# A softmax bound from one column sum per half of the heads, and products with V kept in stock, in an attention and feed-forward kernel on eight cores

## The chip, the cores and the metric

The kernel runs on all eight cores of one Trainium2 chip (two dies of four cores). Each core runs the same program on its own data and none waits for another. The metric is the device time of the slowest core in microseconds (us). Of an execution with a profile, the span is the time from the first to the last instruction on the slowest core; the execution's own time is a little longer.

## What is computed

```python
def attn(x, Wc_down, Wq_up, Wkv_up, Wc_proj):      # 16 heads of 64, one shared K and V
    B, T = (4, 2048)                               # overwritten below: x is (2, 8192, 1024)
    Bsz, Tlen, C = x.shape
    latent = x @ Wc_down                           # 1024 -> 512
    q = (latent @ Wq_up).reshape(Bsz, Tlen, 16, 64)
    kv = latent @ Wkv_up
    k, v = (kv[..., :64], kv[..., 64:])
    att = jnp.einsum('bthd,bsd->bhts', q, k) / 8
    att = jnp.where(causal, att, -jnp.inf)
    att = jax.nn.softmax(att, axis=-1)
    y = jnp.einsum('bhts,bsd->bthd', att, v).reshape(Bsz, Tlen, C)
    return y @ Wc_proj

def ffn(x, w_gate, w_up, w_down):                  # int32 weights times 1/127, hidden 3072
    h = silu(x @ wg.T) * (x @ wu.T)
    return h @ wd.T

xn = layernorm(x)
out = x + attn(xn) * silu(ffn(xn))
```

## The kernel before

**Shares.** Cores 0 to 3 take the first batch row and cores 4 to 7 the second. A core normalizes all 8192 rows of its batch row in 64 tiles of 128 rows (L409, L413), turns them (L241 into `xnT`), and makes keys `kT` and values `vaug` from them in 16 groups of 512. Of each group it owns 128 queries, one **slot**; it computes attention for its 16 slots and the feed-forward part for the same 2048 rows, in four blocks of 512.

**Attention by units.** A slot has four head groups (`hg`) of four heads, and each runs over the keys so far in **units** of 256 keys: `full` ones, then two diagonal ones, `dA` and `dB`, which are multiplied by a mask. There are 1088 units. One unit is (1) scores, four matmuls into two PSUM banks, contraction over 64 rows, where the two halves of the array's rows work side by side (`ps<-qT,kT`, L940; all matmuls are recorded at the helper's line, L230); (2) one exponential on ScalarE, 128x1024, to a slot of the ring `p_sb` (six slots) or, for `dB`, `p_dg` (two slots) (L957); (3) for the diagonal ones the mask, on VectorE or GpSimd (L965); (4) the product with V, eight matmuls of 65 columns (`ps<-vaug,p_sb`, L990), all summed in bank 6. After the last unit of a head group VectorE divides (L1008, L1010), and the next head group's first product waits for that.

**The bound.** The exponential takes a bias per query and half of the heads, `nbias`, instead of a maximum found from the scores: minus a bound that comes from |q| and the greatest |k|. Per slot (`gen_q`) GpSimd squares the queries (L561); four matmuls of 512 columns with a matrix of ones in one half of its rows (`halves_sb`) sum them over partitions, one for each half of the heads and each partition half; VectorE takes the greatest of each (L570), then the greater of two (L582), and then does seven small operations (L583 to L592).

**Order of the work.** All orders are fixed when the program is built. A planner steps through the program in TensorE's order and keeps an estimated time for each engine. At each step it looks at what could come next: scores of two units, or three when a third pair of banks (4 and 5) is lent (`nbuf == 3`), which is done only when no other work is near; the product with V of the oldest unit; the generators in `work` (queries, keys and values, projections); and `lazy`, the feed-forward part. The first of them that is ready by the estimates is taken, in this order. LayerNorm and the ends of the feed-forward part run in the background, on the other engines. Banks 4, 5 and 7 serve all that is not attention (`take`, `give`). When all scores are out (`nu == NU`) the feed-forward part uses longer forms (`gen_down_alone`). Feed-forward weights come over rings: `wgu_sb` (three slots) and `wdr` (eleven).

## Time and profile before

| | us |
|---|---|
| median of 3 runs | 1488.38 (1488.12 to 1488.52) |
| execution with the profile | 1486.96 |
| its span, slowest core (0) | 1485.4; the other cores 1476.2 to 1483.6 |
| TensorE busy with matmuls | 1366.6 (92% of the span) |
| ScalarE busy | 1198.4 (81%) |
| VectorE busy | 690.0 (46%) |
| GpSimd busy | 198.6 (13%) |

Busy times of the engines overlap. A busy TensorE is not one at its peak, since the ends of matmuls are modelled and include what they wait for inside the pipeline. A row of the timeline merges equal instructions that follow each other; the time from its start to the start of the next row of the same engine says more than its length. Where a row names what ended an idle time, that is inferred from semaphores. Some matmul records are missing (of 144 in a row, 141 may stand).

### The profile page before, as it was taken

What the parts mean: (1) busy time and instruction counts of PE and PEld (TensorE: products, weight loads), DVE (VectorE), ACT (ScalarE), POOL (GpSimd) and SP (SyncE); (2) the same over time, 40 slices, a digit from 0 to 9 for tenths busy, and PEclk for the clock granted to TensorE, in tenths of its full rate; (3) what the DMA queues carried; (4) which work ended last, traced back from release to release, by engine and by line L of the source; (5) the groups of instructions that cost most, each with busy time, mean ns of one, the idle gap of its engine ahead of it and who ended that gap; (6) DMA issues with size and microseconds to landing.
All of it is one profiled execution on the core that took longest, in us unless ns stands there. A gap on an engine that the chain in (4) does not pass through costs nothing.

```text
span 1485.4 us, 44737 instructions; the slowest of 8 cores (1476.2 to 1485.4 us)
## 1 busy us (share of the span) xinstructions
PE 1366.6 (92%) x17929; PEld 799.7 (54%) x18064; DVE 690.0 (46%) x1321; ACT 1198.4 (81%) x1254; POOL 198.6 (13%) x352
## 2 busy tenths in 40 slices
PE   2689998899999899999998999999999899999998
PEld 2555555555555556555555555555555555555553
DVE  3678765677574535535334134333332323333325
ACT  3576676777879797997987997998999799998971
POOL 3322122222212212001001012000000112000000
PEclk9899999999999999999999999999999999999999
DMA  9825555476848463421221332421223043212113
GB/s 235 149 86 134 138 111 152 126 184 141 212 124 243 106 198 95 129 73 68 91 79 38 108 104 91 128 73 44 73 73 119 23 140 122 72 64 82 58 45 106
DMA packets 64762, 164.68 MB, mean 111 GB/s; under 512 B 7728, under 2 KB 15152, under 8 KB 64560
## 3 DMA queue, kind: packets, MB, share of 16 engines
q1 hardware_dynamic: 52272, 131.26, 27.3%
q0 software_dynamic: 12288, 30.54, 11.2%
q8 instruction: 149, 2.44, 0.7%
q14 instruction: 53, 0.43, 0.1%
HBM read 151.42 MB, written 33.55 MB: 125 GB/s over the span
## 4 chain that ended last, share of the span: by engine, by line
PE 74%; ACT 8%; issue 7%; DVE 5%; DMA 4%; POOL 1%; DVEq 0%; ACTq 0%; SPq 0%; POOLq 0%
PE ps L230 73%; ACT p_sb L957 6%; DMA h_sb<-wkv 2%; PE ps L241 2%; DVE bnd L570 1%; ACT p_dg L957 1%; POOL p_dg L965 1%; DMA wgub<-wgu_sb 1%; DMA xt<-xb 1%; DVE g_sb L708 1%; DMA wdr<-wd 1%; DVE xnT L473 0%; DVE xn L413 0%; ACT xnT L470 0%; ACT xn L409 0%
## 5 line engine op out<-in xcount | busy, mean ns | idle before, releaser
L957 ACT ACTIVATE p_sb<-ps,nbias 128x1024 bf16<-128x1024 f32 x1024 | 1064.0, 1124 | 150.3 <-PE ps L230 149.7
L230 PEld LDWEIGHTS ps<-vaug,p_sb 128*128 128x128 bf16 x8192 | 310.1, 97 | 190.9 <-issue 154.5
L230 PE MATMUL ps<-vaug,p_sb 128*128 128x65 bf16 x8192 | 386.7, 194 | 24.6 <-DVE p_sb L965 10.1
L230 PE MATMUL ps<-own_f,wgu_sb 128*128 128x512 bf16 x1536 | 393.3, 380 | 7.2 <-DVE g_sb L708 2.1
L230 PE MATMUL ps<-qT,kT 64*128 64x256 bf16 (+1 forms) x4352 | 331.5, 270 | 15.1 <-DVE xnT L473 4.1
L230 PEld LDWEIGHTS ps<-qT,kT 64*128 64x128 bf16 x4352 | 165.0, 94 | 218.7 <-issue 197.5
L230 PE MATMUL ps<-wdr,h_sb 128*128 128x512 bf16 x696 | 182.8, 380 | 5.6 <-DMA wdr<-wd 0.4
L230 PEld LDWEIGHTS ps<-own_f,wgu_sb 128*128 128x128 bf16 x1536 | 126.2, 97 | 109.5 <-issue 11.8
L708 DVE COPY g_sb<-ps 128x512 f32<-128x512 f32 x96 | 66.2, 690 | 190.7 <-PE ps L230 190.1
L710 ACT ACTIVATE t_sb<-g_sb 128x512 f32<-128x512 f32 x96 | 60.8, 634 | 55.3 <-DVE g_sb L708 51.3
L230 PEld LDWEIGHTS ps<-wdr,h_sb 128*128 128x128 bf16 x768 | 62.5, 98 | 50.5 <-issue 4.1
L723 DVE TENSOR_TENSOR h_sb<-g_sb,ps 128x512 bf16<-128x512 f32 x96 | 66.0, 688 | 49.0 <-PE ps L230 45.5
L720 DVE SCALAR_TENSOR_TENSOR g_sb<-t_sb,g_sb 128x512 f32<-128x512 f32 x96 | 66.3, 690 | 46.1 <-ACT t_sb L710 46.1
L965 DVE TENSOR_TENSOR p_sb<-p_sb,mask_sb 128x512 bf16<-128x512 bf16 x63 | 28.8, 456 | 119.5 <-ACT p_sb L957 119.5
L561 POOL TENSOR_TENSOR sq_sb<-qT 128x1024 bf16<-128x1024 bf16 x16 | 31.3, 1956 | 264.5 <-DVE qT L554 143.9
L241 PE MATMUL ps<-ident_sb,xn 128*128 128x128 bf16 x512 | 39.6, 227 | 25.8 <-ACT xn L409 16.4
L230 PE MATMUL ps<-wproj_sb,yT 128*128 128x512 bf16 x235 | 60.8, 379 | 1.1
L768 DVE COPY acc_sb<-ps 128x512 f32<-128x512 f32 x28 | 19.3, 690 | 88.3 <-PE ps L230 88.3
L873 POOL TENSOR_TENSOR acc_sb<-acc_sb,xo_t 128x512 f32<-128x512 f32 x24 | 30.3, 1261 | 177.9 <-DVE acc_sb L870 171.1
L965 POOL TENSOR_TENSOR p_dg<-p_dg,mask_sb 128x512 bf16<-128x512 bf16 x11 | 15.0, 1365 | 283.9 <-ACT p_dg L957 283.9
L241 PEld LDWEIGHTS ps<-ident_sb,xn 128*128 128x128 bf16 x512 | 32.1, 102 | 28.8 <-issue 27.5
L381 DVE BATCH_NORM_STATS2 st<-xt 128x6 f32<-128x512 f32 x57 | 38.9, 683 | 16.8 <-DMA xt<-xb 16.8
(100 smaller groups left out, 996.2 us busy)
## 6 DMA issues: line engine op xcount, KB each, us to landing
wgu_sb<-wgub SPq DMA_DIRECT2D x72, 512.0 KB, 3.4
xt<-xb SPq DMA_DIRECT2D x57, 512.0 KB, 6.0
wdr<-wdb SPq DMA_DIRECT2D x72, 256.0 KB, 3.7
wgu_sb<-wgu POOLq DMA_DIRECT2D x24, 512.0 KB, 7.7
wgub<-wgu_sb SPq DMA_DIRECT2D x24, 512.0 KB, 7.0
out<-acc_sb POOLq DMA_DIRECT2D x28, 256.0 KB, 3.5
wdr<-wd POOLq DMA_DIRECT2D x24, 256.0 KB, 8.4
wdb<-wdr SPq DMA_DIRECT2D x24, 256.0 KB, 8.1
```

What stands on the lines that cost most here:

```text
L230: return p.op("tensor", lambda e: e.matmul(out, lhsT, rhs, start=start, stop=stop, skip_group_check=shared), waits, "pe" if tok else None, ...
L241: return p.op("tensor", lambda e: e.transpose(out, in_, ident_sb[:, :]), waits, "pe" if tok else None, 56.0)
L381: V(600, lambda e, xs=xs, s6=s6: e.bn_stats(s6[:, 0:6], xs[:, 0:512]), [x_tok[j], nrm_tok.get(j - 8)])
L561: sq = P(2200, lambda en: en.tensor_tensor(sq_sb[:, :], qf, qf, ALU.mult), [qe, sq_free[0]])
L708: gc = V(690, lambda e, gv=gv, bg=bg: e.tensor_copy(gv, bank(bg)), [mm, g_free[gr]])
L710: th = A(480, lambda e, gv=gv: e.activation(t_sb[:, :], gv, AF.Tanh, scale=SIG / 2.0), [gc, t_free[0]])
L720: h1 = V(690, lambda e, gv=gv: e.scalar_tensor_tensor(gv, t_sb[:, :], 1.0, gv, ALU.add, ALU.mult), [th])
L723: h2 = V(690, lambda e, gv=gv, bu=bu, m=m: e.tensor_tensor(h_sb[:, m, :], gv, bank(bu), ALU.mult), [h1, mm] + h_free)
L768: accd[tt] = V(690, lambda e, av=av, bd=bd: e.tensor_copy(av, bank(bd)), [mm, acc_free[tt]])
L873: o = (V if over else P)(690 if over else 1200, lambda en: en.tensor_tensor(av, av, res, ALU.add), [u2, t_res])
L957: ex = A(cost, lambda en, dst=dst, src=src, bias=bias: en.activation(dst, src, AF.Exp, bias=bias, scale=0.125), [mm, p_prior(u)[1], bias_t ...
L965: ex = (V if on_v else P)(430 if on_v else 1150, lambda en, mk=mk: en.tensor_tensor(mk, mk, mask_sb[:, :].rearrange("p (a n) -> p a n", n= ...
```

## The change

The changed kernel does five things.

1. **One sum per half of the heads.** The matrix of ones is read shifted by 64 columns (`halves_sb[:, 64:192]`), so that one matmul of 512 columns gives the sum over the lower rows in one half of the output partitions and over the upper rows in the other. Two matmuls and two VectorE maxima per slot are left of four and four. The maxima are written in bfloat16 (`bndb`), and a matmul of two columns with an identity turned by 64 (`ident_sb[:, 64:192]`) exchanges the halves; VectorE then takes the greater of the two, reading PSUM. A factor 1.01 covers the rounding.
2. **Products with V in stock.** The product of the oldest unit is offered first only when five or more (`KEEP`) could run in a row, or the last unit of a head group is within reach. Otherwise it is offered after all other work and the feed-forward part.
3. **Single units.** Scores of one unit alone may be taken when the feed-forward part is done, or when (with two pairs of banks) the scores still to come, at 985 ns each, make more than the TensorE work that is left, with a margin of 40 us.
4. **Rings.** `p_sb` has seven slots instead of six, `wdr` ten instead of eleven.
5. The identity that is loaded is 64 columns wider.

```diff
-DR = 11
-PR = 6
+DR = 10
+PR = 7
+PE_WORK = 1195e3
+SPARE = 40e3
+KEEP = 5
...
             for half in range(2):
-                for o in range(2):
-                    yield lambda: max(ready(sq, t_hv), bank_t())
-                    b, fr = take()
-                    mm = MM(bank(b), halves_sb[:, o * 128:(o + 1) * 128],
-                            sq_sb[:, half * 512:(half + 1) * 512], True, True,
-                            [sq, t_hv] + fr, tok=True)
-                    red = V(690, lambda en, b=b, half=half, o=o: en.reduce_max(
-                        bnd[:, par, half * 2 + o:half * 2 + o + 1], bank(b), axis=AX.X),
-                        [mm, bnd_free[par]])
-                    give(b, [red])
+                yield lambda: max(ready(sq, t_hv), bank_t())
+                b, fr = take()
+                mm = MM(bank(b), halves_sb[:, 64:192], sq_sb[:, half * 512:(half + 1) * 512], True, True,
+                        [sq, t_hv] + fr, tok=True)
+                red = V(690, lambda en, b=b, half=half: en.reduce_max(
+                    bndb[:, par, half:half + 1], bank(b), axis=AX.X), [mm, bnd_free[par]])
+                give(b, [red])
             sq_free[0] = mm
-            yield lambda: ready(kmx_tok.get(e))
+
+            yield lambda: max(ready(red, kmx_tok.get(e)), bank_t())
+            b, fr = take()
+            turned = MM(bank(b)[:, 0:2], ident_sb[:, 64:192], bndb[:, par, :], True, True, [red, t_id] + fr, tok=True)
...
-            a = V(265, lambda en: en.tensor_tensor(pr, q2[:, :, 0], q2[:, :, 1], ALU.max), [red])
+            a = V(265, lambda en, b=b: en.tensor_tensor(pr, bank(b)[:, 0:2], bndb[:, par, :], ALU.max), [turned])
+            give(b, [a])
...
+            single = lazy.done or nbuf == 2 and (NU - nu) * 985.0 + SPARE > PE_WORK - p.pe_work + (NU - nu) * 100.0
...
-                    if n >= 2 and tn > t0:
+                    if n >= (1 if single else 2) and tn > t0:
...
-                if n >= 2 or n and (nu + n == NU or units[nu + n][0] > units[nu][0]):
+                if n >= 2 or n and (single or nu + n == NU or units[nu + n][0] > units[nu][0]):
                     offer(at, ("s", n))
-            if na < nu:
+
+            kept_av = 0
+            while na + kept_av < nu and av_t(na + kept_av) <= t0 and not units[na + kept_av][5]:
+                kept_av += 1
+            if na < nu and (kept_av >= KEEP or units[min(na + kept_av, NU - 1)][5]):
                 offer(av_t(na), ("v", na))
             for w in work:
                 offer(w.at(), ("w", w))
             if not lazy.done:
                 offer(lazy.at(), ("w", lazy))
+            if na < nu:
+                offer(av_t(na), ("v", na))
```

In the two built programs TensorE has 534 runs of score matmuls before (512 of two units, 21 of three, one of one) and 566 in the changed kernel (482, 20 and 64). When the product of a unit stands in TensorE's order, two or three younger units have been scored for 919 of the 1088 units before; in the changed kernel five or more for 588, and fewer than two for 40 (before: 144). Halfway through TensorE's work, counted by matmul columns (scores by half, since two run side by side), 528 units are scored before and 492 in the changed kernel; of the 2304 matmuls of the feed-forward part 920 are done before and 1016 in the changed kernel.

**First place: a diagonal pair in the middle of the program (about 722 us in the profile), on TensorE.** `ps<-qT,kT` are scores (a row of 128x128 is the `dB` unit), `ps<-vaug,p_sb` and `ps<-vaug,p_dg` products with V, `own_f,wgu_sb` and `wdr,h_sb` the two parts of the feed-forward part. Before:

```order
L230 MATMUL ps<-qT,kT 128x256 x8
L230 MATMUL ps<-vaug,p_sb 128x65 x16
L230 MATMUL ps<-own_f,wgu_sb 128x512 x8
L230 MATMUL ps<-qT,kT 128x128 x4
L230 MATMUL ps<-qT,kT 128x256 x4
L230 MATMUL ps<-vaug,p_sb 128x65 x16
L230 MATMUL ps<-qT,kT 128x256 x8
L230 MATMUL ps<-vaug,p_dg 128x65 x8
L230 MATMUL ps<-own_f,wgu_sb 128x512 x6
```

The same `dB` unit in the changed kernel:

```order
L237 MATMUL ps<-qT,kT 128x256 x4
L237 MATMUL ps<-qT,kT 128x128 x4
L237 MATMUL ps<-vaug,p_sb 128x65 x8
L237 MATMUL ps<-wdr,h_sb 128x512 x2
L237 MATMUL ps<-vaug,p_sb 128x65 x8
L237 MATMUL ps<-wdr,h_sb 128x512 x4
L237 MATMUL ps<-qT,kT 128x256 x8
L237 MATMUL ps<-vaug,p_sb 128x65 x40
L237 MATMUL ps<-qT,kT 128x256 x8
L237 MATMUL ps<-vaug,p_dg 128x65 x8
```

Before, the products of two units (16 matmuls) and one run of scores lie between the scores of the `dB` unit and its product; in the changed kernel the products of seven units, six matmuls of 512 columns and two runs of scores.

**Second place: the bound of the last slot (about 1169 us), on TensorE.** `sq_sb,halves_sb` are the sums, `bndb,ident_sb` the exchange. Before:

```order
L230 MATMUL ps<-vaug,p_sb 128x65 x16
L230 MATMUL ps<-sq_sb,halves_sb 128x512 x3
L230 MATMUL ps<-vaug,p_sb 128x65 x16
L230 MATMUL ps<-qT,kT 128x256 x12
L230 MATMUL ps<-sq_sb,halves_sb 128x512
L230 MATMUL ps<-vaug,p_sb 128x65 x8
L230 MATMUL ps<-wdr,h_sb 128x512 x4
```

In the changed kernel:

```order
L237 MATMUL ps<-sq_sb,halves_sb 128x512 x2
L237 MATMUL ps<-qT,kT 128x256 x4
L237 MATMUL ps<-vaug,p_sb 128x65 x8
L237 MATMUL ps<-own_f,wgu_sb 128x512 x2
L237 MATMUL ps<-qT,kT 128x256 x4
L237 MATMUL ps<-vaug,p_sb 128x65 x8
L237 MATMUL ps<-bndb,ident_sb 128x2
L237 MATMUL ps<-own_f,wgu_sb 128x512 x2
L237 MATMUL ps<-qT,kT 128x256 x4
```

The row of three units (x12), which needs banks 4 and 5, stood between the sums and is gone from here; single units stand around the sums, and the exchange comes two units after them.

**Third place: the end of the program, on TensorE.** `wproj_sb,yT` is the projection of the last slot. Before:

```order
L230 MATMUL ps<-qT,kT 128x256 x4
L230 MATMUL ps<-vaug,p_sb 128x65 x16
L230 MATMUL ps<-wdr,h_sb 128x512 x4
L230 MATMUL ps<-vaug,p_sb 128x65 x8
L230 MATMUL ps<-wdr,h_sb 128x512 x6
L241 MATMUL ps<-ident_sb,y_sb 128x128 x4
L230 MATMUL ps<-wdr,h_sb 128x512 x4
L230 MATMUL ps<-wproj_sb,yT 128x512 x16
L230 MATMUL ps<-wdr,h_sb 128x512 x144
```

In the changed kernel (before these rows the first two repeat; in all, 14 single units follow the last matmul of the feed-forward part):

```order
L237 MATMUL ps<-qT,kT 128x256 x4
L237 MATMUL ps<-vaug,p_sb 128x65 x8
L237 MATMUL ps<-qT,kT 128x256 x4
L237 MATMUL ps<-vaug,p_sb 128x65 x32
L248 MATMUL ps<-ident_sb,y_sb 128x128 x4
L237 MATMUL ps<-wproj_sb,yT 128x512 x16
```

The 144 matmuls that followed the last scores stand earlier, among the units, and the program ends with the attention of the last slot.

## Rows read from the trace of the kernel before

**Rows 1.** The page: busy time, share and instructions of each engine.
```profile
PE 1366.6 (92%) x17929; PEld 799.7 (54%) x18064; DVE 690.0 (46%) x1321; ACT 1198.4 (81%) x1254; POOL 198.6 (13%) x352
```

**Rows 2.** Busy time by stretch: from:to, length, engines (instructions), clock, DMA share, GB/s.
```profile
50.00:300.00 250.00, 222.33 (x3053) 141.00 (x3075) 180.65 (x384) 174.41 (x183) 58.53 (x108) 0.98 0.52 126
300.00:700.00 400.00, 373.20 (x5137) 223.74 (x5178) 222.32 (x428) 327.19 (x341) 71.73 (x136) 0.99 0.52 141
700.00:1443.00 743.00, 717.09 (x9383) 403.08 (x9444) 243.60 (x432) 672.22 (x704) 49.64 (x46) 1.00 0.25 81
```

**Rows 3.** Waits of PE from 50 to 1443: waited for, us in total, times, longest.
```profile
PE ps L230 <- ACT p_sb L957: 11.7, 33, 1.3
PE ps L230 <- DVE p_sb L965: 10.1, 18, 1.1
PE ps L230 <- DVE y_sb L1010: 6.5, 8, 2.4
...
PE ps L230 <- POOL p_dg L965: 5.8, 9, 0.8
PE ps L230 <- DVE bnd L570: 4.3, 7, 3.0
PE ps L230 <- DVE den L1008: 3.6, 6, 1.3
```

**Rows 4.** Timeline of PE at the first place: start, length, what, idle before.
```profile
725.12 0.42 PE L230 MATMUL ps<-vaug,p_sb 128*128 128x65 bf16 x8
...
726.09 0.40 PE L230 MATMUL ps<-vaug,p_sb 128*128 128x65 bf16 x8 [0.55 <-DVE p_sb L965]
...
727.70 0.40 PE L230 MATMUL ps<-vaug,p_dg 128*128 128x65 bf16 x8 [0.67 <-POOL p_dg L965]
```

**Rows 5.** Timeline of PE in a steady stretch.
```profile
1002.51 1.03 PE L230 MATMUL ps<-own_f,wgu_sb 128*128 128x512 bf16 x4
1003.47 0.61 PE L230 MATMUL ps<-qT,kT 64*128 64x256 bf16 x8
1004.01 0.67 PE L230 MATMUL ps<-vaug,p_sb 128*128 128x65 bf16 x16
1004.51 1.89 PE L230 MATMUL ps<-own_f,wgu_sb 128*128 128x512 bf16 x8
1006.34 0.61 PE L230 MATMUL ps<-qT,kT 64*128 64x256 bf16 x8
```

**Rows 6.** Groups by line, the bound's maxima: count, busy, mean ns, idle before.
```profile
L570 DVE TENSOR_REDUCE bnd<-ps 128x1 f32<-128x512 f32 x64 | 40.8, 682 | 5.1 <-PE ps L230 5.0
```

**Rows 7.** Timeline of PE at the second place.
```profile
1174.82 0.94 PE L230 MATMUL ps<-qT,kT 64*128 64x256 bf16 x12 [2.98 <-DVE bnd L570]
```

**Rows 8.** Timeline of ACT, PE and DVE at the end of the program.
```profile
1424.43 16.19 ACT L957 ACTIVATE p_sb<-ps,nbias 128x1024 bf16<-128x1024 f32 x16
...
1438.30 0.39 PE L230 MATMUL ps<-qT,kT 64*128 64x256 bf16 x4
1438.62 0.66 PE L230 MATMUL ps<-vaug,p_sb 128*128 128x65 bf16 x16
...
1441.09 0.41 PE L230 MATMUL ps<-vaug,p_sb 128*128 128x65 bf16 x8
...
1443.71 3.62 PE L230 MATMUL ps<-wproj_sb,yT 128*128 128x512 bf16 x16
...
1447.17 31.24 PE L230 MATMUL ps<-wdr,h_sb 128*128 128x512 bf16 x141
...
1482.31 0.69 DVE L873 TENSOR_TENSOR acc_sb<-acc_sb,xt 128x512 f32<-128x512 f32 x1
```

**Rows 9.** Waits of ACT, 50 to 1443; and groups by form, 700 to 1443.
```profile
ACT p_sb L957 <- PE ps L230: 149.7, 147, 5.4
...
L957 ACT ACTIVATE p_sb<-ps,nbias 128x1024 bf16<-128x1024 f32 x604 | 624.2, 1128 | 46.6 <-PE ps L230 46.3
```

**Rows 10.** The page, DMA issues of the first block's weights: KB each, us to landing.
```profile
wgu_sb<-wgu POOLq DMA_DIRECT2D x24, 512.0 KB, 7.7
...
wdr<-wd POOLq DMA_DIRECT2D x24, 256.0 KB, 8.4
```

More of the change, by code:

```diff
@@ L67, in __init__ @@
         self.only_pe = {}
+        self.pe_work = 0.0
         self.T = {"tensor": 0.0, "vector": 0.0, "scalar": 0.0, "gpsimd": 0.0, "sync": 0.0}
@@ L85, in op @@
         self.T[engine] = t
+        if engine == "tensor":
+            self.pe_work += cost
         if dma:
@@ L142, in build_program @@
     wd_d = nc.dram_tensor("wd", [24, 128, 1024], I32, kind="ExternalInput")
-    ident_d = nc.dram_tensor("ident", [128, 128], BF16, kind="ExternalInput")
+    ident_d = nc.dram_tensor("ident", [128, 192], BF16, kind="ExternalInput")
     halves_d = nc.dram_tensor("halves", [128, 256], BF16, kind="ExternalInput")
@@ L161, in build_program @@
     teffv = sbuf("teffv", [128, DK, HD], BF16)
-    ident_sb = sbuf("ident_sb", [128, 128], BF16)
+    ident_sb = sbuf("ident_sb", [128, 192], BF16)
     halves_sb = sbuf("halves_sb", [128, 256], BF16)
@@ L195, in build_program @@
     bnd = sbuf("bnd", [128, 2, 12], F32)
+    bndb = sbuf("bndb", [128, 2, 2], BF16)
     nbias = sbuf("nbias", [128, 2, 2], F32)
@@ L240, in TP @@
         def TP(out, in_, waits=(), tok=False):
-            return p.op("tensor", lambda e: e.transpose(out, in_, ident_sb[:, :]),
+            return p.op("tensor", lambda e: e.transpose(out, in_, ident_sb[:, 0:128]),
                         waits, "pe" if tok else None, 56.0)
@@ L291, in build_program @@
         load_x(1)
-        t_id = DMA(ident_sb[:, :], ident_d[:, :], "c_id", 32)
+        t_id = DMA(ident_sb[:, :], ident_d[:, :], "c_id", 48)
         t_wc = DMA(wc_sb[:, :, :], wc_d.ap().rearrange("(k p) l -> p k l", p=128), "w_c", 2048, engine="gpsimd")
@@ L563, in gen_q @@
             for half in range(2):
-                for o in range(2):
-                    yield lambda: max(ready(sq, t_hv), bank_t())
-                    b, fr = take()
-                    mm = MM(bank(b), halves_sb[:, o * 128:(o + 1) * 128],
-                            sq_sb[:, half * 512:(half + 1) * 512], True, True,
-                            [sq, t_hv] + fr, tok=True)
-                    red = V(690, lambda en, b=b, half=half, o=o: en.reduce_max(
-                        bnd[:, par, half * 2 + o:half * 2 + o + 1], bank(b), axis=AX.X),
-                        [mm, bnd_free[par]])
-                    give(b, [red])
+                yield lambda: max(ready(sq, t_hv), bank_t())
[5 more added lines that the diff above has]
+                give(b, [red])
             sq_free[0] = mm
-            yield lambda: ready(kmx_tok.get(e))
+            yield lambda: max(ready(red, kmx_tok.get(e)), bank_t())
+            b, fr = take()
+            turned = MM(bank(b)[:, 0:2], ident_sb[:, 64:192], bndb[:, par, :], True, True, [red, t_id] + fr, tok=True)
             B = bnd[:, par, :]
-            q2 = B[:, 0:4].rearrange("p (h o) -> p h o", o=2)
             pr = B[:, 4:6]
@@ L581, in gen_q @@
             t = B[:, 8:10]
-            a = V(265, lambda en: en.tensor_tensor(pr, q2[:, :, 0], q2[:, :, 1], ALU.max), [red])
-            a = V(265, lambda en: en.tensor_scalar(pr, pr, kmx[:, e + 1:e + 2], 1.0 / 128.0,
+            a = V(265, lambda en, b=b: en.tensor_tensor(pr, bank(b)[:, 0:2], bndb[:, par, :], ALU.max), [turned])
+            give(b, [a])
+            a = V(265, lambda en: en.tensor_scalar(pr, pr, kmx[:, e + 1:e + 2], 1.01 / 128.0,
                                                    ALU.mult, ALU.mult), [a, kmx_tok[e]])
@@ L1253, in stage_shared @@
         "wgu": np.ascontiguousarray(wgu), "wd": np.ascontiguousarray(wdt),
-        "ident": np.eye(128, dtype=ml_dtypes.bfloat16),
+        "ident": np.concatenate([np.eye(128), np.eye(128)[:, 0:64]], axis=1).astype(ml_dtypes.bfloat16),
         "halves": halves.astype(ml_dtypes.bfloat16),
```

## The prediction

> **What bounds the kernel now.** I read the shares first [rows 1]: TensorE 92%, ScalarE 81%, everything else under half. Then the stretches [rows 2]. From 50 to 300 us TensorE is idle for 27.7 us (250.00 less 222.33), from 300 to 700 for 26.8, from 700 to 1443 for 25.9: 80.4 us in all, in which the change could act. ScalarE's share rises over the same stretches from 70% over 82% to 90%. So TensorE carries the time, with ScalarE close behind it in the last half, and what must be found is how much of TensorE's 80 us the new order takes away and whether ScalarE lets it.
>
> The waits say what TensorE stood for [rows 3]. The largest kind is the input of a product with V: the exponential 11.7 us, the mask on VectorE 10.1, the mask on GpSimd 5.8, together 27.6. Next comes the division between two head groups (6.5 for the quotient, 3.6 for the reciprocal: 10.1), then the maxima of the bound, which keep a PSUM bank that TensorE wants (4.3, once 3.0). A product stands close behind its scores, and every delay on ScalarE goes straight into TensorE's order.
>
> **The change part by part.**
>
> *Bound.* Removed: 32 matmuls of 512 columns. A run of four feed-forward matmuls costs 1.83 us (1004.51 to 1006.34, eight) less 0.96 (1002.51 to 1003.47, four) = 0.87, so 0.217 each [rows 5]: 32 x 0.217 = 6.9 us, all on TensorE's path. Also 32 maxima of 682 ns [rows 6], 21.8 us of VectorE, which is not on the path by itself (46% busy); it counts only through the banks it holds. There TensorE waited 2.98 us for three pairs of banks while the maxima were read [rows 7]. Of the 4.3 us I take 3 away, since half of the readings are gone and that row of three units with them. Added: 16 matmuls of two columns. No row has such a matmul; the nearest is a product with V, 16 in 0.50 us [rows 5], 0.03 each, and above it the start of a score run from rest, 0.09 (below). Bounds 0.5 to 1.4 us; I take 1.0. Added too is a wait: the exchange waits on TensorE for VectorE's second maximum, and scores and feed-forward matmuls are queued behind it. Today the maxima made TensorE wait 7 times in 64 readings, 0.6 us in the mean. With 16 exchanges, bounds are 0 and 16 x 3.0 = 48 us (the longest wait each time); since the planner puts other work between them, I stay near the mean row: three waits, 2 us.
>
> *Stock.* At the first place [rows 4] the eight matmuls from 725.12 to the next start at 726.09 took 0.97 us where eight take 0.25 [rows 5]: 0.72 lost, beside 0.55 in the row. What a wait costs is about 1.2 times its row, because the loading of weights behind it is late too. So 27.6 x 1.2 = 33 us lie in these waits. In the changed order seven units' products lie between instead of two, and units with fewer than two younger ones fall from 144 to 40, so I take nine tenths away: 30 us. What remains is the last unit of a head group, which is urgent in both. Of the 10.1 us of division waits I take half, 5: work now goes ahead of the next group's first product, but that product is sometimes all there is. Bounds for both together: 15 (only the exponential's row goes, the masks stay late) and 43.
>
> *Score runs.* 566 runs instead of 534. A run of eight costs 0.54 (1003.47 to 1004.01) and a run of four 0.32 (1438.30 to 1438.62) [rows 5, 8]: four matmuls 0.22, so 0.10 is fixed. Before it, four feed-forward matmuls took 0.96 instead of 0.87: 0.09 more on entering. 32 x 0.19 = 6.1 us added.
>
> These rows show that a change between 64-row and 128-row matmuls costs 0.19 us for the way in and out. The Trainium skill speaks against more such runs: TensorEngine Tiling, "Key Properties", says that changing the tiling mode drains TensorE, and TensorE: Matmul & The Clock Gate, "Single matmul latency", puts about 166 ns of warm latency on a matmul that cannot hide its drain. An estimate from these pages is 32 x 2 x 0.166 = 10.6 us instead of 6.1, and the forecast would be 4.5 us later. The trace has the duration, so I go by the rows.
>
> *End.* Before, the last score unit is followed by 144 feed-forward matmuls; ScalarE has done its last exponential at 1440.6 (1424.43 + 16.19) and the span ends at 1485.4 [rows 8]. TensorE ends at 1478.4 (1447.17 + 31.24); 7.0 us follow. In the changed kernel the last product is followed by division, turning and projection: 1441.09 to 1447.3 is that chain, 6.2 us, of which TensorE works about 3.9, so 2.3 are idle. Behind it two VectorE operations of 0.69 and an output DMA through GpSimd remain; its landing has no row here, the end of the old kernel (1483.0 to 1485.4, 2.4 us) is a lower bound, and I take 5.4 in all. The 14 single units cost TensorE 0.32 + 0.09 + 0.25 = 0.66 us each, while ScalarE needs 1.01 (16.19 / 16): 0.35 x 14, say 4.5 since some carry two products. Together 2.3 + 5.4 + 4.5 less 7.0 = 5.2 us added.
>
> *ScalarE.* The changed order has 36 fewer units scored halfway. That is 36 us of exponentials moved into a half in which ScalarE was already 672 of 743 us busy [rows 2]. In return it may work almost to the end: its 45 us of rest there shrink to about 12. Work after 700 becomes about 672 + 33 = 705. If TensorE alone decided, the stretch from there to the last exponential would be about 754 us, which leaves ScalarE 49 us of idling; before it had 71, 46.6 of them waiting for scores [rows 9]. Scores no longer stand behind a waiting product, so part of that goes; I charge 8 us, between 0 (all of it goes) and 20 (none).
>
> *Rings.* Seven slots of `p_sb` are what carries a stock of five and a pair; without them scores would wait. One `wdr` slot less is 1.7 us less lead (it feeds two matmuls for each of four tiles, 8 x 0.217); no wait of weight in the rows is for it. Both at nothing. The wider identity is nothing at the start.
>
> **Sum**, against the profiled span of 1485.4: -6.9 + 1.0 - 3 + 2 - 30 - 5 + 6.1 + 5.2 + 8 = -22.6, a span of 1462.8. The median of the runs lies 3.0 above this span (1488.4 to 1485.4), so **1466 us**.
>
> **The rivals.**
>
> *ScalarE keeps its idling (20%).* For it speaks 90% busy after 700 [rows 2], and that the order asks for more in that half. Then its stretch stays 705 + 71 long; only what is saved ahead of 700 (about 12 us) is left of the gain: span about 1474, 1477 us. In the trace of after, the exponential's wait for TensorE would stay near 46 us behind 700.
>
> *More goes than the rows of waits show (18%).* The rows shown name 42 us [rows 3] of the 80; shorter kinds and late weight loads come beside them. If the waits on banks and on feed-forward evictions shrink too, since VectorE has 22 us less and products can be put in between, 43 instead of 35 us go and ScalarE charges nothing: about 1450 us.
>
> *The waits only move (5%).* Scores wait for PSUM banks and a ring slot instead of products for the exponential. Of the 35 us then all but some 5 stays out, and against it stand the other terms without ScalarE's, -6.9 + 1.0 - 3 + 2 + 6.1 + 5.2 = 4.4: about 1488 us.
>
> *The first block's weights come late (12%), the slower side.* The feed-forward part is now taken ahead of products, so it starts earlier, in the stretch with DMA share 0.52 and the most VectorE work (180.65 of 250) [rows 2]. Its 48 first loads take 7.7 and 8.4 us to land, through GpSimd's queue [rows 10], and the ring of `wgu_sb` has three slots. A block of 16 matmuls is 3.5 us, so three slots cover 10.4. Against it: no wait for weights is among the rows now. It decides once the 48 loads are late by more than 0.5 us each (22.6 / 48); at 1 us each, 48 us are added: 1466 + 48 less what the stock can fill, about 1490 to 1510.
>
> **How the numbers follow.** Forecast, 1456 to 1471: 45%. The four rivals 20, 18, 5 and 12%. The range reaches from the larger gain, with its own spread (1446), over ScalarE's case to the edge of no gain (1488); outside lie the late weights and the tail of the larger gain, under 2 in 10. A difference of 0.2% (3 us) is about what a measurement can tell here. Faster: forecast, larger gain, ScalarE's case, 0.83. Within 0.2%: most of the fifth case, 0.05. Slower: 0.12.
>
> **What would show it.** In the changed profile TensorE's waits for `p_sb` and `p_dg` should fall from 27.6 to a few us; those for the quotient and reciprocal to about 5; the groups should have 32 maxima and 16 matmuls of two columns; ScalarE's last exponential should end some 12 us ahead of the end, and its share should pass 92% behind 700 us. The forecast fails if TensorE waits for weights ahead of 300 us, if the exchange shows more than 5 us of waits, or if ScalarE's waits for scores do not fall.

## The result and the profile after

The changed kernel takes 1439.9 us (1439.2 to 1440.0) against 1488.4: a ratio of 0.967 (95% interval 0.965 to 0.969), 48.5 us less. The forecast was 1466 us and a range down to 1446. The sign was right; the gain is a little over twice what the sum gave, and the time lies below the range. In some executions the cores of one die ran at a lower granted clock (the changed kernel once, 1501.1 us at 0.91 to 0.93); these are left out, and all times are medians of the others. The profiled execution took 1439.2 us, with a span of 1437.6 us on core 4. On two other chips the ratio was 0.964 and 0.965.

The page of the changed kernel, first its busy times (answers [rows 1]), then the two groups of TensorE that changed most, and the groups of the same kinds in the kernel before, which were not shown ahead (columns: line, operation, count | busy us, mean ns | idle us before them):

```profile
PE 1354.6 (94%) x18048; PEld 819.6 (57%) x18048; DVE 674.8 (47%) x1294; ACT 1198.0 (83%) x1254; POOL 200.8 (14%) x357
...
L237 PE MATMUL ps<-own_f,wgu_sb 128*128 128x512 bf16 x1536 | 384.8, 380 | 3.9 <-DVE den L1016 2.5
L237 PE MATMUL ps<-vaug,p_sb 128*128 128x65 bf16 x8192 | 359.9, 194 | 18.4 <-ACT p_sb L965 6.4
```

```profile
L230 PE MATMUL ps<-vaug,p_sb 128*128 128x65 bf16 x8192 | 386.7, 194 | 24.6 <-DVE p_sb L965 10.1
L230 PE MATMUL ps<-own_f,wgu_sb 128*128 128x512 bf16 x1536 | 393.3, 380 | 7.2 <-DVE g_sb L708 2.1
```

Busy time by stretch, as in [rows 2]; the last stretch ends with the span, at 1437.6:

```profile
50.00:300.00 250.00, 231.49 (x3070) 146.52 (x3069) 179.97 (x382) 172.96 (x183) 59.14 (x114) 0.97 0.62 147
300.00:700.00 400.00, 384.85 (x5227) 234.42 (x5228) 225.49 (x425) 327.85 (x342) 70.23 (x129) 0.99 0.49 141
700.00:1443.00 743.00, 718.63 (x9550) 422.02 (x9547) 246.83 (x442) 677.55 (x710) 54.73 (x55) 0.99 0.25 82
```

TensorE is idle for 18.5, 15.2 and 19.0 us, 52.7 where [rows 2] had 80.4. The 19.0 hold the 7.4 us behind its last matmul; before, 7.0 such us lay in a stretch of their own, so that 45.3 is the number to compare.

The 80.4 can't be taken as they stand either. On the core that [rows 1] and [rows 2] show, 135 of 18064 matmul records are missing (17929, beside 18064 weight loads), and a missing record counts as idle time. In the trace of the changed kernel none is missing on core 4. Core 5 of the same execution of before has all of them too, with a span of 1483.6 us:

```profile
PE 1377.8 (93%) x18064; PEld 799.9 (54%) x18064; DVE 688.8 (46%) x1321; ACT 1199.5 (81%) x1254; POOL 198.7 (13%) x352
...
50.00:300.00 250.00, 224.77 (x3084) 140.24 (x3082) 180.34 (x384) 175.40 (x184) 58.23 (x105) 0.98 0.51 127
300.00:700.00 400.00, 378.00 (x5181) 223.89 (x5178) 221.54 (x429) 328.24 (x342) 71.34 (x137) 0.99 0.51 141
700.00:1443.00 743.00, 720.76 (x9436) 403.04 (x9436) 243.99 (x433) 671.28 (x702) 49.61 (x46) 1.00 0.25 82
```

There 69.5 us of idle time became 45.3. Over the whole span idle time fell from 105.8 to 83.0 us and busy time from 1377.8 to 1354.6. **Half of the 46.0 us between these two cores, 23.2, is busy time.** By the prices of the rows little of that is work: 6.9 us of sums less, 6.1 of score runs more, about 0.5 for the exchange, 1.3 for the slower projection at the end. That leaves, as an estimate, some 24 us that stood as busy and were delays.

The group of products, 359.9 us of busy time instead of 386.7 with the same 8192 instructions, is a poor witness of them. A record of 194 ns, of which some 30 are the spacing to the next start, reaches 0.16 us over whatever follows. Before, the products stand in 746 uninterrupted runs in TensorE's order, in the changed kernel in 632. So 114 x 0.16, some 18 of these 27 us, is only overlap with other groups that went because the runs are longer. A trace with an unchanged order follows below.

Waits of TensorE from 50 us on (answers [rows 3]):

```profile
PE ps L237 <- ACT p_sb L965: 12.5, 36, 0.9
PE ps L237 <- DVE p_sb L973: 4.1, 6, 1.7
PE ps L237 <- DVE y_sb L1018: 3.9, 4, 1.9
...
PE ps L237 <- DVE den L1016: 2.7, 6, 0.9
PE ps L237 <- DVE bndb L576: 2.6, 1, 2.6
PE ps L237 <- DMA wdr<-wd: 2.3, 2, 1.8
...
PE ps L237 <- POOL p_dg L973: 1.3, 3, 0.5
```

The masks' waits fell from 15.9 to 5.4. The exponential's did not fall (11.7 before, 12.5 now), so the three rows of products' inputs make 17.9 us instead of 27.6, where the prediction looked for a few. Quotient and reciprocal make 6.6 instead of 10.1 (about 5 expected). Of the exponential's 12.5 a third (4.3 us in 13 pieces) lies in the last 15 us of attention, where ScalarE sets the pace. The first place, with the same `dB` unit as in [rows 4]:

```profile
733.94 0.61 PE L237 MATMUL ps<-qT,kT 64*128 64x256 bf16 x8
734.48 1.39 PE L237 MATMUL ps<-vaug,p_sb 128*128 128x65 bf16 x40
735.81 0.61 PE L237 MATMUL ps<-qT,kT 64*128 64x256 bf16 x8
736.35 0.42 PE L237 MATMUL ps<-vaug,p_dg 128*128 128x65 bf16 x8
736.60 1.46 PE L237 MATMUL ps<-wdr,h_sb 128*128 128x512 bf16 x6
```

40 products take 1.33 us from start to the next start, 33 ns each, and the product of the masked unit waits for nothing. The second place (answers [rows 7]), and below it the maxima of the bound (answers [rows 6]):

```profile
1168.64 0.39 PE L237 MATMUL ps<-qT,kT 64*128 64x256 bf16 x4
1168.97 0.42 PE L237 MATMUL ps<-vaug,p_sb 128*128 128x65 bf16 x8
1169.22 0.17 PE L237 MATMUL ps<-bndb,ident_sb 128*128 128x2 bf16 x1
1169.25 0.59 PE L237 MATMUL ps<-own_f,wgu_sb 128*128 128x512 bf16 x2
```

```profile
L576 DVE TENSOR_REDUCE bndb<-ps 128x1 bf16<-128x512 f32 x32 | 20.6, 684 | 1.3 <-PE ps L237 1.3
```

The exchange takes 0.03 us of TensorE's order (1169.22 to 1169.25). It made TensorE wait 2.6 us once in 16 times. A single unit costs 0.33 us to the next start (1168.64 to 1168.97), as the rows of before gave.

The end (answers [rows 8]), PE, ACT and DVE:

```profile
1409.32 0.40 PE L237 MATMUL ps<-qT,kT 64*128 64x256 bf16 x4
1409.55 13.21 ACT L965 ACTIVATE p_sb<-ps,nbias 128x1024 bf16<-128x1024 f32 x13
...
1414.86 0.39 PE L237 MATMUL ps<-qT,kT 64*128 64x256 bf16 x4 [0.26 <-ACT p_sb L965]
...
1422.90 0.40 PE L237 MATMUL ps<-vaug,p_sb 128*128 128x65 bf16 x8 [0.60 <-ACT p_sb L965]
...
1425.33 4.90 PE L237 MATMUL ps<-wproj_sb,yT 128*128 128x512 bf16 x16 [0.68 <-DVE yT L1035]
...
1432.38 0.54 POOL L261 DMA_DIRECT2D out<-own_f  x1 [1.11 <-DVE own_f L1065]
```

ScalarE sets the pace of the last 13 units, 1.02 us each. Its last exponential ends at 1422.8, 14.9 us ahead of the end. From the start of these 13 units to the end of the span TensorE is idle for 13.4 us; in the last 61 us of before it was for 7.4. The projection took 4.90 us instead of 3.62 [rows 8]; TensorE had waited 0.60, 0.60, 0.97 and 0.68 us in pieces before it, and the granted clock stood at its lower level (1.2 instead of 2.4 GHz) from 1424.6 to 1427.9 (busy time by stretch; the third number from the end is the clock's share):

```profile
1424.60:1427.90 3.30, 2.62 (x8) 0.95 (x8) 0.42 (x1) 0.00 (x0) 0.00 (x0) 0.50 0.00 0
1428.00:1431.00 3.00, 2.23 (x11) 0.78 (x8) 2.05 (x3) 0.00 (x0) 0.27 (x1) 1.00 0.00 0
```

ScalarE's exponentials from 700 us on (answers [rows 9]):

```profile
L965 ACT ACTIVATE p_sb<-ps,nbias 128x1024 bf16<-128x1024 f32 x611 | 631.8, 1128 | 32.5 <-PE ps L237 31.6
```

They waited 31.6 us for scores instead of 46.3, with more of them in the stretch.

Last, the chain of waits from 50 to 1420 us, of before and then of after, shares by engine and line. The rest of each line is smaller:

```profile
by line: PE ps L230 74.1%; issue 7.0%; ACT p_sb L957 6.9%; PE ps L241 1.5%; DVE bnd L570 1.1%; ACT p_dg L957 0.8%; POOL p_dg L965 0.8%; DMA wgub<-wgu_sb 0.8%; DMA xt<-xb 0.7%; DVE g_sb L708 0.7%; DMA wdr<-wd 0.7%; DVE xnT L473 0.5%; DVE xn 
```

```profile
by line: PE ps L237 85.7%; ACT p_sb L965 3.2%; issue 2.3%; PE ps L248 2.2%; DMA xt<-xb 1.6%; DMA wdr<-wd 1.0%; DVE p_dg L973 0.4%; ACT xn L416 0.3%; POOL p_dg L973 0.3%; ACT xnT L477 0.3%; ACT p_dg L965 0.3%; DVE g_sb L716 0.3%; DVE st L388
```

Before, 24% of this stretch, some 330 us, was not TensorE's own work on the chain. The exponential and "issue" alone, the latter being handovers for which the profile shows no wait, had 14%, 190 us; after, 5.5%. All that isn't TensorE's own fell to 12%, some 166 us. Such shares say who held up whom, not what can be gained: they fell by 168 us, the span by 48.

### The profile page after: what moved, and what is told of

Read it like the earlier page. It is cut to its first block, busy times and chain, and to the rows that moved or that the text cites. A ratio compares the mean times of both kernels' runs of the same rounds, so it can differ in the third digit from the quotient of the medians.

```text
span 1437.6 us, 44760 instructions; the slowest of 8 cores (1427.5 to 1437.6 us)
## 1 busy us (share of the span) xinstructions
PE 1354.6 (94%) x18048; PEld 819.6 (57%) x18048; DVE 674.8 (47%) x1294; ACT 1198.0 (83%) x1254; POOL 200.8 (14%) x357
## 4 chain that ended last, share of the span: by engine, by line
PE 85%; DMA 5%; ACT 4%; DVE 3%; issue 2%; POOL 0%; ACTq 0%; DVEq 0%; SPq 0%; POOLq 0%
PE ps L237 83%; ACT p_sb L965 3%; PE ps L248 2%; DMA h_sb<-wkv 2%; DMA xt<-xb 2%; DMA wdr<-wd 1%; ACT xnT L477 0%; DVE p_dg L973 0%; ACT xn L416 0%; POOL p_dg L973 0%; ACT p_dg L965 0%; DVE g_sb L716 0%; DVE st L388 0%; DVE st L391 0%; DVE p_sb L973 0%
## 5 line engine op out<-in xcount | busy, mean ns | idle before, releaser
L237 PE MATMUL ps<-own_f,wgu_sb 128*128 128x512 bf16 x1536 | 384.8, 380 | 3.9 <-DVE den L1016 2.5
L237 PE MATMUL ps<-vaug,p_sb 128*128 128x65 bf16 x8192 | 359.9, 194 | 18.4 <-ACT p_sb L965 6.4
L237 PE MATMUL ps<-wdr,h_sb 128*128 128x512 bf16 x768 | 197.2, 383 | 3.7 <-DMA wdr<-wd 2.3
L237 PE MATMUL ps<-wproj_sb,yT 128*128 128x512 bf16 x256 | 67.2, 386 | 0.7 <-DVE yT L1035 0.7
L870 DVE SCALAR_TENSOR_TENSOR acc_sb<-t_sb,acc_sb 128x512 f32<-128x512 f32 x30 | 20.8, 692 | 63.3 <-ACT t_sb L868 63.3
L388 DVE BATCH_NORM_STATS2 st<-xt 128x6 f32<-128x512 f32 x57 | 38.9, 682 | 17.9 <-DMA xt<-xb 17.9
```

Source lines behind the costliest of these rows:

```text
L237: return p.op("tensor", lambda e: e.matmul(out, lhsT, rhs, start=start, stop=stop, skip_group_check=shared), waits, "pe" if tok else None, ...
L388: V(600, lambda e, xs=xs, s6=s6: e.bn_stats(s6[:, 0:6], xs[:, 0:512]), [x_tok[j], nrm_tok.get(j - 8)])
```

## The experiments

All ratios are to the kernel before, run beside the others on the same chip (where it took 1491.9 to 1496.0 us). Two chips apart, one kernel's ratio differs by up to 0.003.

### Is it the products' inputs?

**Theory A**: the masks and exponentials for which products wait cost far more than the rows show. I compared, for each run of products, when its first weights were loaded with when the run before it should have ended by the spacings of undisturbed rows. Products came 80 us late in sum before and 33 us after. These sums hang on what counts as undisturbed: with the spacing that a third of the equal places in the traces stay under, the same loads come 45 and 16 us late. **Theory B**: the rows times 1.2, as in the prediction. The edit takes the inputs away and keeps the order:

```diff
-                    ws = [p_tok[u], v_tok[t // 4]] + (av_free if first else [])
-                mm = MM(ps[:, c:c + 65], pv[:, blk * 128:(blk + 1) * 128], vaug[:, t + tt, 0:65],
+                    ws = [t_hv, v_tok[t // 4]] + (av_free if first else [])
+                mm = MM(ps[:, c:c + 65], halves_sb[:, 0:128], vaug[:, t + tt, 0:65],
...
+                        planned=p_tok[u] if i == 0 else None)
```

(`planned` goes into the planner's estimate alone. The exponential waits in addition for the mask that last wrote its slot.)

> The kernel before with every order kept word for word, but each product with V takes a constant tile (the matrix of ones) as its stationary operand and doesn't wait for its exponential or mask; these still run, so the output is not that of the reference. It measures what the waits for a product's inputs cost in the order of before. Theory A (many short waits that the rows of idle time do not show, since a matmul's recorded end covers up to some 0.2 us of a wait): loading starts of the products in the trace of before come 80 us late in sum, so about 1488 - 75 = 1413 us. Theory B (the rows of idle time times 1.2, as in the prediction): 1488 - 33 = 1455 us, and the rest of the gain of the change has another cause.

> The same edit in the changed kernel (constant tile, no wait for exponential or mask, order kept, output not that of the reference). Theory A: products' loads come 33 us late in its trace between 50 and 1400 us, so 1440 - 30 = 1410 us, close to what the same edit gives in the kernel before, since both orders hold nearly the same TensorE work. Theory B: the rows name 12.5 + 4.1 + 1.5 + 1.3 = 19 us, 12 of which lie at the end: 1440 - 20 = 1420 us, some 35 us under the kernel before with the same edit.

Measured: in before's order 1474.6 us, ratio 0.987 (0.986 to 0.989); in the changed order 1437.7, 0.962 (0.961 to 0.964), 3 to 5 us under the changed kernel's own ratio (0.964 and 0.965) on other chips. **Both theories fall.** Without any wait for a product's input, before's order is only 20 us faster, and the changed order still beats it by 37. (By the second way of counting, lateness ahead of products falls from 45 to 24 us in before's order, close to the 20 gained.) The groups of TensorE show why. Of before, and then with free inputs:

```profile
L230 PE MATMUL ps<-vaug,p_sb 128*128 128x65 bf16 x8192 | 386.7, 194 | 24.6 <-DVE p_sb L965 10.1 <-ACT p_sb L957 6.6 <-DVE y_sb L1010 5.9
L230 PE MATMUL ps<-qT,kT 64*128 64x256 bf16 (+1 forms) x4352 | 331.5, 270 | 15.1 <-DVE xnT L473 4.1 <-ACT p_sb L957 3.9 <-DVE bnd L570 3.0
```

```profile
L230 PE MATMUL ps<-vaug,halves_sb 128*128 128x65 bf16 x8704 | 397.2, 194 | 6.1 <-DVE y_sb L1013 5.7 <-issue 0.2
L230 PE MATMUL ps<-own_f,wgu_sb 128*128 128x512 bf16 x1536 | 393.0, 380 | 17.2 <-DVE den L1011 4.1 <-DVE g_sb L708 4.1 <-POOL ksq_sb L497 3.4
L230 PE MATMUL ps<-qT,kT 64*128 64x256 bf16 (+1 forms) x4352 | 336.8, 270 | 23.2 <-ACT p_sb L958 8.0 <-DVE xnT L473 5.5 <-DVE bnd L570 4.1
```

The idle time ahead of products went from 24.6 to 6.1 us; that ahead of feed-forward matmuls rose from 7.2 to 17.2 and ahead of scores from 15.1 to 23.2. The three add up to 46.9 and 46.5. The idle time of these groups changed its place and nothing else. What the span lost, 1485.4 to 1474.1 us, is busy time of TensorE, 1366.6 to 1353.8. Since order, rows and missing records are the same in both traces, this shows the hidden delays: all 8704 products (both tiles together, before and then with free inputs) are busy for 11.4 us less. On all eight cores it is 408.0 to 408.6 against 396.9 to 398.0.

```profile
0.00:1500.00 1500.00, 408.61 (x8704) 328.85 (x8704) 6.74 (x16) 0.27 (x1) 0.99 0.39 110
0.00:1500.00 1500.00, 397.24 (x8704) 326.98 (x8704) 6.74 (x16) 0.27 (x1) 0.99 0.39 110
```

### Theory E: places at which nothing is ready

That gave another theory. In before's order there are places at which, when the order was made, **nothing was ready**: not a product, not scores, no generator. The planner then takes what will be ready first, and TensorE stands there, for whatever kind comes next. Products are offered first, so they are used up at once, and none is left for such a place. In the changed kernel they are kept and fill it. I counted these places in the planner's own run (the steps in which what it takes is later than its time) and summed what it expects TensorE to stand there, behind the first 50 us. These sums are the planner's estimates, not the chip's times:

| kernel | nothing ready (planner), us | score runs | ratio measured |
|---|---|---|---|
| before | 114 | 534 | 1 |
| before, inputs free, order made anew | 144 | 523 | 1.001 |
| before with the new bound alone | 97 | 533 | 0.988 |
| changed, without stock | 94 | 542 | 0.986 |
| changed, without single units | 90 | 533 | 0.974 |
| changed, old rings | 100 | 633 | 0.989 |
| changed, old bound | 61 | 545 | 0.962 |
| the same, estimate 720 ns | 78 | 543 | 0.978 |
| changed, KEEP 3 | 71 | 566 | 0.972 |
| changed | 60 | 566 | 0.964 to 0.967 |
| changed, rings 9 and 8 | 52 | 555 | 0.955 |

The sums and the times go together, but not row by row: 90 us go with 0.974 and 78 with 0.978. The number of score runs alone does not go with the times (533 at 0.988 and at 0.974).

The test that parts A from E is the second row. If products need no input and the planner knows it, theory A has its best case, while theory E says that they are then taken even earlier and fill nothing.

```diff
-            return max(ready(p_tok.get(u), v_tok.get(t // 4)), ready(*av_free) if first and u else 0.0)
+            return max(ready(v_tok.get(t // 4)), ready(*av_free) if first and u else 0.0)
```

> The kernel before with products that need no input (constant tile, as in b_free_inputs; output not that of the reference), but now the planner knows it and makes a new order with it (its estimate of a maximum is 705 ns instead of 690). Products are then always ready and, being offered first, are taken at once, so that none is left over. Theory A (waits for the products' inputs are what costs): this is the best case, 1450 us or less. Theory E (what costs are places where nothing at all is ready in the order of before, whatever kind comes next, and a product kept back is what fills them): nothing is kept back here either; by the planner's own estimates TensorE then stands 144 us with nothing ready behind the first 50 us, against 114 in before and 60 in the changed kernel, so no faster than b_free_inputs (1474.6 us): 1475 to 1505 us.

Measured: 1495.6 us, ratio 1.001 (0.999 to 1.003). **No gain at all from products that are always ready**, and some 20 us slower than with the same freedom and the old order. That ends theory A. For theory E it is what was expected, but as the sum of two effects, 30 us more planned with nothing ready against the 20 us that free inputs give. TensorE's waits moved to the other producers, from 50 to 1420 us:

```profile
PE ps L230 <- ACT p_sb L958: 19.5, 38, 1.2
PE ps L230 <- DVE xnT L473: 14.3, 7, 2.8
PE ps L230 <- DVE y_sb L1013: 12.8, 15, 1.8
```

The second test leaves all instructions and rules as they are and shifts one estimate, so that another order comes out:

```diff
-                    red = V(690, lambda en, b=b, half=half, o=o: en.reduce_max(
+                    red = V(720, lambda en, b=b, half=half, o=o: en.reduce_max(
```

> The changed kernel with the old bound, and the planner's estimate of one maximum of the bound 720 ns instead of 690: the same instructions, only another order comes out. By the planner TensorE then has 78 us with nothing ready instead of 61. Theory E (these places carry the time): some 13 to 17 us over a_old_bound (ratio 0.9625), so a ratio of 0.972; and then the 5 us between old and new bound are within what an order can shift. If the kinds of rule (stock, single units) carry it and such places don't: the ratio stays within 0.960 to 0.965.

Measured: 1458.4 us, ratio 0.978 (0.974 to 0.981), where the same kernel with 690 had 0.962 twice. 0.015, some 22 us, for nothing but another order of the same instructions. Theory E holds in direction and, a little short, in size (13 to 17 expected).

The planner's places can also be set beside the trace one by one, since the weight loads are complete and each step of the plan is a known number of them. I call a step late by what it exceeds the time that a third of the equal steps (same kind, same neighbours) stay under; this is an estimate. Between 50 and 1400 us, before comes 70 us late at the 280 places that were planned with nothing ready, and 35 us at all 2702 others. The changed kernel comes 30 us late at 113 such places and 21 at the others (on two other chips 30 and 20, 28 and 25). So of some 54 us that went, about 40 lay at planned places and 14 elsewhere, and even at its places the chip stood for less than planned (109 us before).

### What each part gives

The bound alone in the kernel before, and the changed kernel with the old bound (the hunks of `gen_q` of the change, put in or taken out):

> The kernel before with the new bound alone (two sums, two maxima, exchange by the turned identity); rings, stock and single units as before. The prediction's terms: -6.9 + 1.0 - 3 + 2 = -6.9 us, so 1481.5 us. If VectorE's 22 us of maxima had held up much more than the rows show (banks, masks and evictions behind them), 1470 us or less. If the exchange's wait costs what it could, up to 1495 us.

> The changed kernel with the old bound (four sums, four maxima): stock, single units and rings alone. If the two parts add up, about 1440 + 7 = 1447 us, a gain of 41 us over before from the stock with its rings and single units. If the new bound is what makes the stock work (fewer banks held), 1460 us or more.

Measured: 1476.3 us, 0.988 (0.987 to 0.990), a gain of 18 us for the bound alone instead of 7; and 1436.9 us, 0.962 (0.961 to 0.964), so that stock, rings and single units alone give all 57 us. The parts don't add up. Whether the new bound then costs something was tried beside the changed kernel:

> The changed kernel itself, beside the three that follow. On the chip of the last runs the changed kernel with the old bound stood at 0.9625 of the kernel before, while the changed kernel had 0.967 on another chip. If the new bound gains its 7 us also beside the stock, the ratio here is 0.958; if the two parts overlap (each takes away the same waits), it is 0.962 to 0.963; if the difference is one of chips alone, 0.967 against some 0.967 for the old bound.

> The changed kernel with the old bound once more, now beside the changed kernel on one chip. On two chips it stood at 1436.9 and the changed kernel at 1442.5 us, with 1494.3 and 1496.4 us for before. If the new bound adds nothing beside the stock or costs a little (exchange, more single units): 3 to 7 us under the changed kernel. If the chips made the difference: 7 us over it.

> The changed kernel, as the reference for the three beside it: 1440 to 1443 us.

Measured: the changed kernel 1442.4 us (0.964, 0.963 to 0.966) on one chip, and on another 1444.0 us (0.965, 0.962 to 0.968) beside 1439.7 (0.962, 0.960 to 0.965) with the old bound. The intervals overlap; the medians lie 4 us apart. Beside the stock the new bound gives no gain that can be seen. But an order can shift the time by 22 us, so these 4 us can't be laid to the bound.

Then the changed kernel without the stock, without single units, and with the rings of before:

```diff
-            kept_av = 0
-            while na + kept_av < nu and av_t(na + kept_av) <= t0 and not units[na + kept_av][5]:
-                kept_av += 1
-            if na < nu and (kept_av >= KEEP or units[min(na + kept_av, NU - 1)][5]):
+            if na < nu:
                 offer(av_t(na), ("v", na))
...
-            if na < nu:
-                offer(av_t(na), ("v", na))
```

> The changed kernel, but products with V are offered first again, as before (no KEEP, no late offer); bound, single units and rings as in the changed kernel. Theory C (the stock is what gains, by giving TensorE something that is surely ready whenever anything else may be late): back to the level of the bound alone, ratio 0.985 to 0.99. Rival D (single units and the larger ring of exponentials gain, since ScalarE is fed without a break): ratio 0.97 or less.

```diff
-            single = lazy.done or nbuf == 2 and (NU - nu) * 985.0 + SPARE > PE_WORK - p.pe_work + (NU - nu) * 100.0
+            single = False
```

> The changed kernel, but never scores of one unit alone (except where before had them). Theory C: 32 or so score runs fewer give back 6 us, at the end pairs cost some: within 5 us of the changed kernel. Rival D: the gain goes, ratio 0.975 or more.

```diff
-DR = 10
-PR = 7
+DR = 11
+PR = 6
```

> The changed kernel with the rings of before: six slots for exponentials, eleven for w_down. Theory C with the ring as a condition: a stock of five and a pair don't fit in six slots, scores wait for a slot and feed-forward work goes ahead, ratio 0.975 or more. If the stock needs no more than three or four units: within 5 us of the changed kernel.

Measured: without stock 1474.8 us (0.986, 0.984 to 0.988), the level of the bound alone. Without single units 1457.6 (0.974, 0.972 to 0.976): they give 15 us, against my "within 5". With the old rings 1479.1 (0.989, 0.987 to 0.991): nearly the whole gain goes. With six slots a stock of five leaves one free; the planner then makes 199 single units and 633 score runs. TensorE's busy time rises with them, to 1368 to 1376 us on the cores that have all records, against 1349 to 1353 in the changed kernel on that chip, so that some half of this loss is the cost of short runs and not standing with nothing ready. The stock is what gains, a seventh slot is the condition of a stock of five, and single units help it. A smaller stock in six slots, and the stock alone without single units and new bound, were not run.

Size of the stock, and a larger ring:

```diff
-KEEP = 5
+KEEP = 3
```

> The changed kernel with KEEP 3: products are offered first from three ready ones on instead of five. By the planner 71 us with nothing ready instead of 60. Theory E: 8 to 11 us over the changed kernel (ratio 0.965), so 0.971. If a stock of two or three is as good as five, since a wait is shorter than two products: 0.964 to 0.967.

```diff
-DR = 10
-PR = 7
+DR = 8
+PR = 9
```

> The changed kernel with nine slots for exponentials and eight for w_down (KEEP 5 as it is). Theory E: the stock can stay whole while scores of pairs or threes go ahead; the planner has 52 us with nothing ready instead of 60, so some 8 to 11 us less than the changed kernel, 1431 us. If the shorter ring of w_down makes TensorE wait for weights (2.3 us now): no gain or slower.

Measured: KEEP 3 gives 1450.7 us, 0.972 (0.968 to 0.975), as expected. **Nine slots for exponentials and eight for `wdr` give 1427.8 us, 0.955 (0.952 to 0.958)**, beside 1444.0 for the changed kernel on that chip. It beats both kernels, by 16 us against the changed one where 8 to 11 were expected. From 700 to 1420 us TensorE is busy for all but 7.4 us (7.0 in the changed kernel on that chip), so the further gain is not seen there; over the span busy time is 1347.7 us against 1359.3. No wait for weights is among its larger ones. The stretch:

```profile
700.00:1420.00 720.00, 712.61 (x9488) 404.42 (x9486) 244.19 (x434) 672.09 (x705) 51.56 (x51) 1.00 0.26 85
```

## Why the prediction was wrong

- **Stock, -35: the step that failed.** I took the waits of which the rows said that products stood for them, times 1.2, nine tenths of it, and half of the division's. Changed without the stock is 32 us slower than changed, so as a size this term is not far off. But its base was wrong: the stock doesn't take away the waits for inputs (the freed inputs gave 20 us and left all other gains open), it takes away places at which nothing is ready, of every kind. The rows charged with 25 of the 27.6 us lost 9.7 (27.6 to 17.9), while all idle time fell by some 24 us and busy time by 23. Of the 38 us of idle time in [rows 2] that [rows 3] did not name, some 10 are missing records (69.5 us instead of 80.4 on a core that has all).
- **Factor 1.2 per wait.** From two waits at one place [rows 4]. It missed waits of under 0.2 us, which make no row. In before's order those of products held 11 us of busy time (408.6 to 397.2 us with free inputs), and some 24 us of all kinds are an estimate for before and after.
- **Bound, -6.9.** 18 us alone. The work on TensorE (-6.9 + 1.0) stands as a count at the rows' price. Banks and exchange (-3 + 2) were -1, measured -3: before, TensorE waited 6.5 us for the maxima (4.3, and 2.2 ahead of transposes that the prediction left out), with the bound alone 3.5, of which 2.6 for the exchange. Some 9 of the 18 us are thus in neither term, and what they are is not shown; the order changed too. With half of the maxima the order itself has fewer such places (97 instead of 114 us by the planner). Beside the stock it gives nothing visible, which fits if both take away the same places. I had added the parts as if they were apart.
- **Exchange, +2.** 2.6 us, once, where three waits made the 2. Right in sum. Of TensorE's order it takes 0.03 us, where I took 0.06.
- **Score runs, +6.1.** The prices 0.32 and 0.54 us hold in the changed trace. But single units, which I booked as a cost alone, save 15 us. That they do it by letting ScalarE start without waiting for a pair is the likely reason, and not tested by itself. The 10.6 us for their drains, estimated from the two pages of the Trainium skill named in the prediction (TensorEngine Tiling, Key Properties, and TensorE: Matmul & The Clock Gate, Single matmul latency), are not seen; the rows of the changed kernel give 0.19 us per run again, 0.10 inside it (0.33 us for four matmuls, 0.54 for eight) and 0.09 on entering (two feed-forward matmuls ahead of it take 0.52 us, from 1169.25 to 1169.77, instead of 0.43).
- **End, +5.2.** Measured +6.0: 13.4 us of idle time instead of 7.4. TensorE's last matmul ends at 1430.2, and 7.4 us follow, 5.4 taken. The chain to the end of the projection is 7.3 instead of 6.2 us, since the clock fell in it. Single units: 1.02 us each, as said.
- **ScalarE, +8: wrong.** Its stretch from 700 to the last exponential is 722.8 us with 677.6 of work: 45 us of idling, where I said that 49 would be left if TensorE alone decided. It gave way wholly. The work behind 700 us, which I had grow by 33 us to 705, grew by 5: fewer units scored at half of TensorE's columns is not fewer exponentials done at 700 us. The waits for scores fell from 46.3 to 31.6, as the text asked for.
- **The rivals.** ScalarE's case and the late weights did not come: TensorE waited for weights 2.3 us in all, though the DMA share from 50 to 300 rose from 0.52 to 0.62. "More goes than the rows show" (18%) was the right one, and its 1450 us were still short, because it was drawn from the idle rows too, which show nothing of the busy half. The end and the score runs, which it charged in full, cost about what they were said to.

So the mechanism as told (a product close behind its scores passes every delay on) was a part of it. How the gain is shared is known as an estimate alone: some three quarters at places planned with nothing ready, a quarter at others, delays that the plan doesn't know and the stock absorbs. That the planner's 54 us less are so near the measured 49 to 54 is partly luck, since at its places the trace gives 40. What stays open is what stock, single units and the larger ring give each by itself, since each was only taken out of the whole, and what the bound alone gains beyond its terms.

## What to carry to other kernels

When an in-order engine is fed from a fixed order, look for places at which nothing is ready, and not for what is waited for most: remove one input and the wait goes to the next producer. Keep back work whose inputs are long there, and give it a ring that holds stock and batch together: six slots for a stock of five and a pair lost nearly all, seven gained 54 us, nine (with eight for `wdr`) another 16. Before comparing idle times, see that both traces have all their records, and before comparing a group's busy time, in how many runs it stands. An order made by a planner moves by a per cent or more from a small change of one estimate, so a part's worth needs several orders or the count of such places beside the time.

## What the runs showed of the hardware

TensorE's rows hide short waits. The record of a 65-column product lasts 194 ns, and in an undisturbed run the next starts 30 to 33 ns later, so waits of under about 0.16 us (194 less 33) leave no idle time. With the same 8704 products in the same order their busy time was 408.6 us with waits for their inputs and 397.2 without. On one core 135 of 18064 matmul records were missing, on another core of the same execution none, and idle time from 50 to 1443 us read 80.4 and 69.5. A matmul with two moving columns took 0.03 us of the order. Behind waits of 0.60, 0.60 and 0.97 us, TensorE's granted clock stood at 1.2 GHz for some 3.3 us, and 16 projection matmuls took 4.90 us instead of 3.62.
